# First layer by arrival: W1 feature gathers after tile 0's, and a new order of the tile pipeline, in a two-layer recommender kernel

## The reference, cut to what matters

```
cont_emb = emb_table[:13][None, :, :] * conts[:, :, None]
cate_emb = emb_table[cates]
cc = concatenate([cont_emb, cate_emb], axis=1)
pairs = einsum('bfd,bgd->bfg', cc, cc)[:, ROWS, COLS]
X = concatenate([cont_emb, cate_emb, pairs])            # 39*64 + 741 features
X = relu(layernorm(X @ W1 + b1, ln1_g, ln1_b))          # 1024
X = relu(layernorm(X @ W2 + b2, ln2_g, ln2_b))          # 1024
return sigmoid(X @ Wout + bout)
```

## Time and profile before

| | |
|---|---|
| median of 3 runs | 852.54 us (851.6 to 855.34) |
| the profiled execution | 849.3 us, span of the core 847.5 us |
| mean granted TensorE clock | 0.963 |
| PE busy | 787.0 us, 93% of the span |
| DVE, ACT, POOL busy | 486.7, 388.5, 492.7 us |
| chain that ended last | PE 88%, POOL 4%, issue 3%, DVE 3%, ACT 2%, DMA 1% |

### The profile page before, as it was taken

One profiled execution on the slowest core, in us unless ns is written; L12 is line 12 of the kernel. 1 busy time (PEld: TensorE's weight loads), 2 busy tenths in 40 slices (PEclk: granted clock), 3 DMA queues, 4 the chain that ended last, 5 costly groups with the idle time before them and its releaser, 6 DMA issues.

```text
span 847.5 us, 12350 instructions
## 1 busy us (share of the span) xinstructions
PE 787.0 (93%) x4287; PEld 638.2 (75%) x4287; DVE 486.7 (57%) x1050; ACT 388.5 (46%) x735; POOL 492.7 (58%) x458
## 2 busy tenths in 40 slices
PE   6367697999999999999999999999999999999994
PEld 1245586888888888888888888888888788888883
DVE  2444837555565555655556555565556576555666
ACT  0343736354362543625446354463538444455441
POOL 5747774776767667677677767767100143344433
PEclk9686698999999999999999999999999999999998
DMA  9973453647455473554635547364256211111000
GB/s 265 254 169 26 26 25 43 49 28 49 26 49 47 26 48 25 48 48 25 48 26 48 47 26 47 26 48 48 9 181 241 75 27 49 49 49 49 25 1 0
DMA packets 27229, 50.72 MB, mean 60 GB/s; under 512 B 11406, under 2 KB 11662, under 8 KB 27206
## 3 DMA queue, kind: packets, MB, share of 16 engines
q0 software_dynamic: 14992, 16.77, 33.2%
q1 hardware_dynamic: 9478, 24.94, 10.0%
q10 hardware_dynamic: 2736, 8.71, 2.6%
HBM read 41.99 MB, written 8.40 MB: 59 GB/s over the span
## 4 chain that ended last, share of the span: by engine, by line
PE 88%; POOL 4%; issue 3%; DVE 3%; ACT 2%; DMA 1%; ACTq 0%; DVEq 0%; POOLq 0%
PE acc L472 24%; PE acc L474 23%; PE acc L473 23%; PE tr L514 4%; PE gr L553 4%; PE tr L553 4%; POOL xb L435 3%; PE tr L497 1%; PE gr L497 1%; PE gr L648 1%; PE tr L648 1%; POOL raw_lo L421 1%; PE gr L530 1%; PE tr L523 1%; DMA xb<-in_L_rec_emb_table,idx 1%
## 5 line engine op out<-in xcount | busy, mean ns | idle before, releaser
L435 POOL DMA_INDIRECT xb<-in_L_rec_emb_table,idx x416 | 412.6, 992 | 172.3 <-issue 132.1
L472 PE MATMUL acc<-w_hi,x_hl 128*128 128x512 f32 x416 | 176.2, 424 | 7.7 <-DVE w_lo L974 7.7
L474 PE MATMUL acc<-w_hi,x_hl 128*128 128x512 f32 x416 | 165.7, 398 | 0.0
L473 PE MATMUL acc<-w_lo,x_hl 128*128 128x512 f32 x416 | 164.8, 396 | 0.0
L455 POOL TENSOR_TENSOR raw_lo<-raw_lo,raw_hi 128x1024 f32<-128x1024 f32 x15 | 35.9, 2395 | 167.3 <-ACT raw_lo L869 167.3
L718 ACT CAST xg<-x_hl 64x192 fp32r<-64x192 f32 (+1 forms) x192 | 117.2, 610 | 3.0
L472 PE MATMUL acc<-w_hi 128*128 128x512 f32 x256 | 101.0, 395 | 1.4 <-DVE raw_lo L1154 1.4
L474 PE MATMUL acc<-w_hi,w_lo 128*128 128x512 f32 x256 | 99.7, 389 | 0.0
L473 PE MATMUL acc<-w_lo,w_hi 128*128 128x512 f32 x256 | 99.7, 389 | 0.0
L472 PEld LDWEIGHTS acc<-w_hi,x_hl 128*128 128x128 f32 x416 | 79.8, 192 | 25.3 <-DVE w_lo L974 9.4
L474 PEld LDWEIGHTS acc<-w_hi,x_hl 128*128 128x128 f32 x416 | 79.4, 191 | 18.1
(11 more groups left out here) (110 smaller groups left out, 1140.2 us busy)
## 6 DMA issues: line engine op xcount, KB each, us to landing
h_scratch<-h_row ACTq DMA_DIRECT2D x16, 512.0 KB, 5.8
raw_hi<-h_scratch SPq DMA_DIRECT2D x16, 512.0 KB, 3.6
raw_lo<-in_L_rec_W SPq DMA_DIRECT2D x26, 256.0 KB, 13.5
xb<-in_L_rec_emb_table,idx POOLq DMA_INDIRECT x416, 3.6
raw_lo<-in_L_rec_W SPq DMA_DIRECT2D x8, 512.0 KB, 7.0
raw_hi<-in_L_rec_W SPq DMA_DIRECT2D x6, 512.0 KB, 6.9
raw_hi<-in_L_rec_b SPq DMA_DIRECT2D x1, 512.0 KB, 4.2
raw_hi<-in_L_rec_ln_g SPq DMA_DIRECT2D x1, 512.0 KB, 5.1
```

Of the source, the lines that this page charges most:

```text
L435: nc.gpsimd.indirect_dma_start(out=xb[:, f * DIM:(f + 1) * DIM], out_offset=None, in_=emb, in_offset=bass.IndirectOffsetOnAxis(ap=idx[:, p ...
L472: nc.tensor.matmul(o, a, w, start=first, stop=False)
L473: nc.tensor.matmul(o, a, v, start=False, stop=False)
L474: return nc.tensor.matmul(o, b, w, start=False, stop=last)
```

## The change

It does seven things.

1. POOL issues all 26 gathers of tile 0 first and W1's feature rows after them, ahead of tile 1's gathers. k-tile 16's rows come in two DMAs (one for the rows before v, one for those behind, with `w1_tail`), so that v can be written before they land: seven DMAs in place of six.
2. ACT copies v into W1's rows as its first work. SP no longer waits for k-tile 16's rows ahead of b1's row.
3. PE transposes only group 0 before tile 0's k-tiles. `FIRST`, `SECOND` and `STEADY` are new and `LAST` is added for tile 15. "own 1" takes the place of "next 1"; "factor" and "late" of a tile move into the tile after ("factor prev", "late prev"), save in `LAST`; "next 0" is now the last share of a tile.
4. W1's splits are spread in another way over tile 0 (`W1_BEFORE`).
5. ACT and DVE make the copies of group 1 ahead of the split of group 3.
6. Norm 1 of the tile before runs ahead of all four `take_dots`, on DVE ahead of `cate_features` too, in place of between the second and the third.
7. `split_group(x + 1, 1)` and `gram_copies(x + 1, 0)` go behind the factor and late features. `split_group(x + 1, 0)` stays right behind `choose_pairs`.

```diff
-STEADY = (0, "own 2", "own 3", 1, 13, 14, 15, "cont", 16, "gram 0", 17, 18, "gram 1", 2, "gram 2", 3, 4, 5, "gram 3",
-          6, 7, 8, 9, "next 0", "next 1", 10, "factor", 11, "late", 12)
-FIRST = (0, 1, 2, 3, 4, "own 2", 5, 6, 7, 8, "own 3", 9, 10, "cont", 11, "gram 0", "gram 1", 12, "gram 2", "gram 3",
-         "next 0", "factor", "late", "next 1")
-SECOND = (0, 1, 13, 14, 15, 16, 17, 18, 2, 3, "own 2", 4, 5, 6, "own 3", 7, 8, "cont", 9, "gram 0", "gram 1",
-          10, "gram 2", "gram 3", "next 0", "factor", 11, "late", "next 1", 12)
+STEADY = (0, 1, "factor prev", 2, "late prev", "own 1", 3, 13, 14, 15, 16, 4, 17, 5, "own 2", 18, 6, "own 3", 7, 8, "cont", 9,
+          "gram 0", 10, "gram 1", 11, "gram 2", "gram 3", 12, "next 0")
+FIRST = (0, 1, 2, 3, "own 1", 4, 5, 6, "own 2", 7, 8, 9, "own 3", 10, "cont", 11, 12, "gram 0", "gram 1", "gram 2", "gram 3",
+         "next 0")
+SECOND = (0, 1, 2, 3, "factor prev", "late prev", "own 1", 13, 14, 15, 4, 5, 6, "own 2", 16, 17, 18, 7, "own 3", 8, 9, "cont",
+          10, "gram 0", 11, "gram 1", 12, "gram 2", "gram 3", "next 0")
+LAST = (0, 1, "factor prev", 2, "late prev", "own 1", 3, 13, 14, 15, 16, "own 2", 4, 17, "own 3", 18, 5, 6, "cont", 7,
+        "gram 0", 8, "gram 1", 9, "gram 2", "gram 3", 10, 11, 12, "factor", "late")
...
-W1_BEFORE = {"own 1": (0, 1, 2), "own 2": (3, 4, 5), "own 3": (6, 7, 8, 9, 10), "dots 0": (11,), "dots 2": (12,),
-             "choose": (13, 14, 15, 16), "end": (17, 18)}
+W1_BEFORE = {"own 1": (0, 1, 2, 3), "own 2": (4, 5, 6), "own 3": (7, 8, 9), "copies": (10,), "dots": (11, 12),
+             "own 1 next": (13, 14, 15), "end": (16, 17, 18)}
...
-                        if first and f % 4 == 3 and f // 4 < FK:
-                            feature_rows_of(f // 4)
...
             gather(0, 0, first=True)
+            for s in range(NF):
+                feature_rows_of(s)
             gather(1, 1)
...
+            act.wait_ge(v_done, 1)
+            nc.scalar.copy(raw_lo[EK + FT][V_AT:V_AT + CONT, :],
+                           acc[1][0:CONT, :, :].rearrange("p h n -> p (h n)")).then_inc(v_in, 1)
             split_group(0, 0)
             w1_before("own 1")
             split_group(0, 1)
...
+                gram_copies(x, 1)
                 split_group(x, 3)
-                gram_copies(x, 1)
+                if first:
+                    w1_before("copies")
                 gram_copies(x, 2)
+                if first:
+                    w1_before("dots")
+                else:
+                    norm1(x - 1, 1 - par)
+                    h1_store(x - 1)
                 for q in range(FILLS):
-                    if first and q in (0, 2):
-                        w1_before(("dots 0", "dots 2")[q // 2])
-                    if q == 2 and not first:
-                        norm1(x - 1, 1 - par)
-                        h1_store(x - 1)
                     take_dots(x, q, first)
...
                 choose_pairs(x)
                 if not last:
                     split_group(x + 1, 0)
-                    split_group(x + 1, 1)
-                    gram_copies(x + 1, 0)
                 factor_hi(x)
                 late_features_hi(x)
                 tail_features_hi(x)
+                if first:
+                    w1_before("own 1 next")
+                if not last:
+                    split_group(x + 1, 1)
+                if first:
+                    w1_before("end")
+                if not last:
+                    gram_copies(x + 1, 0)
```

More of the change, by code:

```diff
@@ L61 @@
 WHOLE = 5 * DIAG
-FK = 6
-KT = EK + FK
+NF = 6
+FK = NF + 1
+KT = EK + NF
 K2 = HID // P
@@ L119, in feature_rows @@
             rows[DIAG * ((k - 1) % 5) + f, FT + 1 + (k - 1) // 5] = late_row(f, k)
+    rows[0:WHOLE - PART, NF] = rows[PART:WHOLE, FT]
     return rows
@@ L228, in build @@
         v_in = sem("v_in")
+        w1_tail = sem("w1_tail")
         w1_rounded = sem("w1_rounded")
@@ L420, in feature_rows_of @@
                 m = rows_of(EK + s)
[L421 to L424, removed]
+                pieces = ((0, m, s, w1_in[EK + s]),) if s != FT else ((0, V_AT, s, w1_in[EK + s]), (PART, m, NF, w1_tail))
+                for a, b, column, landed in pieces:
+                    nc.gpsimd.indirect_dma_start(
+                        out=raw_lo[EK + s][a:b, :], out_offset=None, in_=W1,
+                        in_offset=bass.IndirectOffsetOnAxis(ap=rows_sb[0:b - a, column:column + 1], axis=0),
+                    ).then_inc(landed, 16)
             def gather(x, par, first=False):
@@ L574, in _ @@
             pe.wait_ge(setup_done, 1)
-            for g in range(2):
-                transpose_group(0, g, first=True)
+            transpose_group(0, 0, first=True)
             def share(x, what, first, last):
-                if what == "own 2":
+                if what == "own 1":
+                    transpose_group(x, 1, first)
+                elif what == "own 2":
                     transpose_group(x, 2)
@@ L593, in share @@
                     transpose_group(x + 1, 0)
-                elif what == "next 1" and not last:
-                    transpose_group(x + 1, 1)
+                elif what == "factor prev":
+                    factor(x - 1)
+                elif what == "late prev":
+                    late(x - 1)
             def k_tile(x, par, kt):
@@ L679, in _ @@
                     iteration(2 * i + (3 + u), 1 - u)
-            iteration(TILES - 1, 1, last=True)
+            iteration(TILES - 1, 1, LAST, last=True)
             product2(1, 1)
@@ L773, in w1_hi_part @@
                     act.wait_ge(w1_up[k], 16)
[L774 to L775 removed]
                 if k == EK + FT:
+                    act.wait_ge(w1_tail, 16)
                     act.wait_ge(b1_in, 16)
[L778 to L779 removed]
                     act.wait_ge(v_in, 1)
```

31 lines of the change are left out of this document (3 added, 28 removed).

## The result

| | before | changed |
|---|---|---|
| median of 4 runs | 852.07 us (851.55 to 855.34) | 929.18 us (926.5 to 929.86) |
| the profiled execution, span | 849.3, 847.5 us | 926.5, 924.7 us |
| mean granted TensorE clock | 0.963 | 0.940 |
| PE busy | 787.0 us, 93% | 809.4 us, 88% |

The changed kernel takes 1.0893 times as long, with a 95% interval of 1.0872 to 1.0914. The forecast was 920, the range 885 to 948.

A forecast was written before the change was run, and what follows sets the result against it. PE bounds the middle of stage one without a gap; only the opening has idle time. 849.3 - 12.7 + 1.0 + 1.8 + 76.7 + 1.3 = 917.4 us; with 3.2 for the median, 920, range 885 to 948.

The forecast's parts named there:

- the seam: Between two tiles, 13 times: PE idles about 4.1 us (3.6 to 4.6) until group 0 is split behind the pairs.
- The links: Chain from "gram 3" to k-tile 0: dots, pairs and sums, `chosen`, cast, low part and handovers, 6.06 us in sum.
- the half clock behind a seam: After each seam's wait PE's clock falls to 0.50, costing 1.8 us per seam, bounds 0 to 3.25.
- rival A: The seam opens but the clock holds: 25 us less, a median of 895; chance 0.13.
- rival B: Each seam's half-clock stretch is busy throughout, 3.25 us in place of 1.8: a median of 940; chance 0.14.
- The mis-sized step: Half-clock cost after two earlier waits, PE busy 3.77 and 3.29 us of 6.5: 1.9 and 1.6 us, taken as 1.8.
- the opening: Up to tile 2's k-tile 0: reached at 126.4 in place of 139.08 us, -12.7, bounds -22 to -3.
- rival C: The opening does not gain: tile 1's gathers, behind W1's seven, come late and take back 12.7, giving 933; chance 0.06.
- I cost this at nothing: W1's seven gathers ahead of tile 1's on POOL: even with a 9.25 us stop, tile 1's start near 58; 0 us.
- the walk of PE: Opening, step by step: k-tile 0 at 27.5, k-tile 10 at 59.6, tile 1's k-tile 0 at 78.2, tile 2's at 126.4.
- the small terms: Ten transposes +1.0, half clock after the second seam +1.8, `LAST` +1.3; norm 1, features behind dots and late group 3 nothing.
- The seams' term: Thirteen steady seams, each a gap of 4.1 plus half clock of 1.8 us: +76.7 us.

The follow-up runs named there:

- Run 10: Changed kernel with group 0 of the next tile split ahead of the pairs, on chip C: 873.4 us, 1.0256 of the kernel before.
- Run 11: Changed kernel with group 0 split ahead of the pairs, padded feature gathers and a k-tile behind "next 0", on chip C: 836.5 us, 0.985 of the kernel before.
- e2_pool_old: Changed kernel with W1's feature gathers back between tile 0's, still seven pieces, on chip B: 1095.33 us, 0.9383 of the kernel before.
- e1_seam: Changed kernel with group 0 of the next tile split ahead of the pairs, on chip B: 1091.99 us, 0.9364 of the kernel before.
- g3_seam: Run 10 by its kernel name: changed kernel with group 0 split ahead of the pairs, chip C, 873.4 us, 1.0256 of the kernel before.

## Why the prediction was right or wrong

**Right: what bounds, and the seam.** PE's wait at each seam was forecast at 4.1 us and is 3.95. The links: dots 1.11 and 0.1, pairs and sums 2.54 (2.64 forecast), `chosen` 0.81 (0.84), cast 0.58 (0.59), low part 0.69 (0.69). The cover that the old order gave PE, k-tiles behind "next 0", was rightly named as the thing lost. Run 10 shows that the cast's place behind the pairs is the cause: moved ahead, it takes 50.6 us back. Run 11 shows the other half: with one k-tile behind "next 0", and the orders changed around it, the remaining 1.40 goes as well.

**Right in kind, too large: the half clock behind a seam.** Forecast 1.8 per seam, measured 1.45. The clock did fall behind every one, so rival A (clock holds, 895) is out; the stretch lasts 3.4 us, so rival B (long stretch, 940) is out too. The 1.45 is what a tile has left over beside the wait; the clock's part of it is 1.35. The mis-sized step took the time that PE is busy at half clock from windows behind two other waits, 3.77 and 3.29 us; behind a seam it is 2.94. 13 x 0.35 = 4.6 us of the difference from the 76.7 forecast, and the gap's 0.15 another 2.0: together the 6.5 between 76.7 and 70.2. The rule of the Trainium skill (TensorE: Matmul & The Clock Gate, section HAM oscillation), throttled time times one half, gives 3.4 / 2 = 1.7 as an estimate. The trace shows less, 1.35; half of the busy part, 2.94 / 2 = 1.47, is nearer.

**Wrong: the opening.** Forecast -12.7, measured +3.3: rival C, to which I gave 0.06, happened, and in this term alone. The failed step is the one that says "I cost this at nothing" of W1's seven gathers ahead of tile 1's. It took the old stop of 9.25 us as the worst such stop, and had tile 1's gathers start near 58. There were two stops, 8.15 and 17.20 us, and tile 1's gathers started at 79.07. I had counted the DMAs (seven in place of six) and never asked how the new one, of 79 rows, would be spread. Up to there the walk of PE held: k-tile 0 at 27.22 (27.5 forecast), the waits for `w_lo` 6.81 and 2.77 (6.9 and 2.9). Then k-tile 10 came at 61.58 (59.6), with one more wait for `w_lo` of 2.11 behind it, and tile 1's k-tile 0 at 94.00 in place of 78.2. That is 15.8 of the 16.0 us missed. From tile 1's k-tile 0 to tile 2's the forecast was 48.2 and it took 48.4.

How the 15.8 us divide can only be estimated. The grams ended at 78.35, for a forecast of 72: W1's own rows came later than forecast, for which ACT waited (2.22, 1.25 and 2.72 us, at 53.91, 63.11 and 66.89; SP issued W1's loads until 53.1), and the clock was at 0.50 through the grams. The second seam takes 6.14 us from the end of "gram 3" to k-tile 0 (136.24 to 142.38), so with the gathers in time tile 1's k-tile 0 would stand near 84.5. It stands at 94.00: some 9.5 are the gathers', as the seam's own wait hides in their 13.04, and some 6.3 what came before. The two do not simply add, though: run 10 shows that PE, there sooner, goes on no sooner. With the gathers in time the opening would by this estimate have been 6 us faster than before and not 12.7, inside my bounds.

The total came out at +77.2 for a forecast of +68.1: +16.0 from the opening, -6.5 from the seams and -0.4 from the small terms (3.7 for 4.1). The seams' term held by its mechanism. That the total came so near was in part luck: two errors ran against each other.

**Right: the small terms.** Norm 1 ahead of the dots, the features behind it and group 3 late cost nothing: no such wait stands in a steady tile. In `LAST`, PE waits 0.23 us for `chosen` and 0.39 for the features.

## What to carry to other kernels

When an order is changed, follow the last result that the next stage needs back through each engine's own queue. What stands between there and the old place is the loss, and it is paid once per iteration; a cast of 0.6 us put ahead of three microseconds of pairs gave back 50 of 77 us. When a transfer is cut in two, look at how many rows each piece has, not only at how many transfers there are: 80 in place of 79 took a stop of some 17 us off the issuing engine here, together with 128 in place of 125. And time a variant beside its base on the same chip, and look at the base's time first: on two of the four chips here the base took 1.37 to 1.39 times as long, and a variant that loses 2.6% elsewhere came out 6% ahead.

## What was not expected of the hardware

- In every program with the indirect gather of 79 rows of 4 KB, POOL stopped for 14.2 to 19.6 us behind it, and in the changed kernel and `e2_pool_old` the DMA share was 0.06 in the later part of the stop. With 80 rows (and 128 for 125) the stop was gone.
- A PE wait of 3.95 us took the granted clock to 0.50 for 3.4 us; one of 1.40 us, in the same place of the same loop, left it at 1.00.
- On chips B and D the kernel before takes 1169 to 1181 us, on the first and C 850 to 853, and the order of the kernels turns. Windows of the same program, `e1_seam` on B and `g3_seam` on C:

```profile
400.00:500.00 100.00, 82.64 (x420) 66.24 (x420) 41.43 (x92) 33.69 (x60) 49.55 (x52) 0.87 0.33 27
```

```profile
400.00:500.00 100.00, 95.80 (x537) 78.21 (x536) 54.04 (x121) 46.49 (x82) 65.86 (x70) 1.00 0.47 34
```

In the same 100 us the first does 420 matmul records where the second does 537. PE stands on "issue" in grams and transposes while POOL gathers, and every trace of B and D has waits of ACT and DVE put down to "remote" (on ACT 306.7 us in `e1_seam`), while none of the first chip or of C has one. Why was not found.
